# Gate and up products of a Mamba-macaron layer as seven block products

## Chip, core and metric

One NeuronCore of a Trainium2 chip. The metric is the device time of one launch in microseconds; lower is better. Three runs of the kernel before gave a median of 832.96 us (832.76 to 834.3).

## What is computed

One layer on 2048 tokens of width 512, all in float32: `x = x + 0.5 * ffn(layernorm(x))`, `x = x + attn(layernorm(x))`, `x = x + 0.5 * ffn(layernorm(x))`. `ffn` is one 512x512 product with a dequantized int4 weight plus a rank 16 term and a bias. `attn` is a Mamba-2 mixer (16 chunks of 128 tokens, 4 heads) and behind it the part that the change touches:

```
h2 = rmsnorm(h, ln2_w)                                    # 2048 x 512
mlp = silu(h2 @ gate_w.T) * (h2 @ up_w.T) @ down_w.T      # 512 -> 1792 -> 512
return h + mlp
```

## The kernel before

A float32 operand of a large product is held as two float16 parts, high and low, and a product is three matmuls (`product`, `PARTS`: high x high, high x low, low x high) for each 128 of the contracted length. All these matmuls have one line, L1382. Producing a pair of parts takes two instructions: ScalarE copies to float16 (high), VectorE subtracts (low).

The engines run queues that are written out by hand, and wait on semaphores. SyncE issues nearly all transfers.

First come the dequantization, the first ffn and the mixer, chunk by chunk (`step(c)`, c = 0 to 15). In chunk c, GpSimd does `scan_c`, `scan_d` and `rms2` (the root mean square of chunk c, and the addition to the rows `xs`); ScalarE squares (`square`), makes `h2n_p` (`hi2`) and exponentials (`scan_ecs`, L591, which TensorE's `s1_mask`, L1465, waits for); SyncE then transposes h2 into the tile `h2`. The 1792 features are taken as 7 pairs of 256 (p = 0 to 6); a pair's gate and up weights are `raw_gu`, its down weights `raw_d`. The weights are multiplied by `ln2` (`fold`), scaled by a power of two found with GpSimd's `pair_max` (a reduction over partitions, L428), and cut in parts (`cut_a`, `cut_b`: L612, L1069, L783, L1080).

For a pair, `gate_up(p, n)` computes for one of 4 tiles i of 512 tokens and one half x of 128 features the gate and the up product: 24 matmuls into two PSUM banks. Then ScalarE takes tanh (L790), VectorE makes silu and the product of the two (L1297, L1298), and the result is cut in parts (L800, L1304). `down(p, i)` multiplies a tile's 256 features by the down weights: 4 chunks of 6 matmuls, each added to `xs` by one VectorE instruction, L1315. So a pair is 8 x 24 + 16 x 6 = 288 matmuls. Four `gate_up` of pair 0 run inside chunks 12 to 15. `gate_up(0, 5)` is the one that needs the h2 of the last chunk.

At the end comes the second ffn: for each of 16 chunks VectorE's statistics (`c_stats`), GpSimd's `c_norm` and `c_bias`, ScalarE's `c_hi`, VectorE's `c_lo`, a transposing transfer, 12 matmuls (`c_f`) and `c_out`. The last pair's `down` for the tiles 2 and 3 run beside its beginning, the ones for 0 and 1 between its `gate_up`.

Of the kernel before, what the change touches and what calls it, by code (L numbers as in the profile page):

```python
# [14 lines left out]
P = 128  # L15
EPS = 1e-5
ACT_SCALE = 2.0 ** 10
DOWN = ACT_SCALE ** -2
GATED_SCALE = 2.0 ** -54
W_TOP = 14  # L20
# [8 lines left out]
def build(nc, x_in, w_in_t, conv_w, conv_b, a_log, d_skip, dt_bias, w_out_t, ln1_w, ln2_w,  # L29
# [23 lines left out]
    with ctx:  # L53
# [29 lines left out]
        w_dn = [n_T[:, 1024 * p:1024 * (p + 1)].rearrange("p (b n) -> p b n", b=2) for p in range(2)]  # L83

# [18 lines left out]
        state = sb("state", [P, H, P])  # L103

# [23 lines left out]
        d_diag = sb("d_diag", [P, H, P])  # L128
# [80 lines left out]
        def tokens_of(t, c):  # L209
# [30 lines left out]
            sem(n) for n in "e_h2T e_xres e_ncs e_gu e_tanh_g e_silu_g e_gated e_gated_hi".split())  # L240
        e_gated_lo, e_down, e_acc, e_w_gu0, e_w_gu1d, e_w_hi, e_fold, e_wmax = (
# [42 lines left out]
        def _(sp_):  # L284
# [61 lines left out]
            for c in range(NCH):  # L346
                a = c + 2 * CH
                if a + 1 < NCH:
                    t0(a + 1)
                if c > 0:  # L350
                    t2(c - 1)
                if a < NCH:
                    t1(a)
                    next_x(a)
            t2(NCH - 1)
            for p in range(1, NP):
                sp_.wait_ge(e_w_gu1d, p * 2)
                load_pair(p)
# [18 lines left out]
        def _(po):  # L377
# [116 lines left out]
            def step(c):  # L494
# [37 lines left out]
        def _(ac):  # L532
# [134 lines left out]
            def step(c):  # L667
# [35 lines left out]
                if c == 2 * CH + 2:  # L703
                    cut_a(0)
                if c == 2 * CH + 3:
                    cut_b(0)
# [71 lines left out]
            def cut_b(p):  # L778
                if p > 0:
                    ac.wait_ge(e_gu, p * (2 * NS))  # L780
                    ac.wait_ge(e_down, p * (NS * CH))
                hi_gu(1)
                ac.activation(w_dn[0], raw_d[:, :, :], ACT.Copy, scale=sw3[:, 2:3]).then_inc(e_w_hi, 1)  # L783

            def gate(p, n):
                s = p * (2 * NS) + n
                k = order_of(p)[n]
                ac.wait_ge(e_gu, s + 1)
                ac.wait_ge(e_descale, p + 1)
                ac.activation(gt[:, n % 2, :], bank(gu_bank(p, n, 0)), ACT.Tanh, scale=dgh[:, :]).then_inc(e_tanh_g, 1)  # L790
                ac.wait_ge(e_gated, s + 1)
                if k >= NS:
                    i = k - NS
                    if i >= 2:
                        if p * (NS * CH) + (i - 1) * CH > 0:
                            ac.wait_ge(e_down, p * (NS * CH) + (i - 1) * CH)
                    dst = mB[0][:, i % 2, :]
                else:
                    dst = mA[0][:, k, :]
                ac.activation(dst, gp[:, n % 2, :], ACT.Copy).then_inc(e_gated_hi, 1)  # L800
# [6 lines left out]
            def pair(p, nxt):  # L807
                for n in range(EARLY_GU if p == 0 else 0, 2 * NS):
                    gate(p, n)
                    if p > 0 and n == 0:  # L810
                        cut_b(p)
                    if nxt and n == 2 * NS - 2:
                        cut_a(p + 1)

            for p in range(NP):
                pair(p, p + 1 < NP)
# [13 lines left out]
        def _(ve):  # L830
# [362 lines left out]
            def step(c):  # L1193
# [38 lines left out]
                if c == 2 * CH:  # L1232
                    fold(0)
                if c == 2 * CH + 1:
                    maxima_gu()
# [4 lines left out]
                if c == 2 * CH + 3:  # L1240
                    cut_a(0)
# [6 lines left out]
                else:  # L1248
                    if j == 0:
                        cut_b(0)  # L1250
# [470 lines left out]
```

## Time and profile before

| | |
|---|---|
| median of 3 runs | 832.96 us |
| the profiled execution | 831.91 us, of which the span shown is 830.2 us |
| TensorE busy | 95% of the span |
| VectorE, ScalarE, GpSimd busy | 69%, 39%, 23% |
| mixer and the chunks, up to TensorE's last `w(15)` | until 365.8 us |
| seven pairs | until 785.3 us |
| second ffn | until the end |

A row of the timeline has start and duration in us, engine, line, operation, output and inputs, the count, and in brackets the idle time before it with what ended it. A group row has shapes, count, total busy us, the mean ns of one, and the idle time before. Matmuls are pipelined: their distance, and not the length of one, is what a row of many costs.

### The profile page before, as it was taken

The numbers are of one execution on the slowest core, as the hardware profiler recorded it, in microseconds if no ns is written. First come the engines' busy times: TensorE is split into PE (matmuls) and PEld (weight loads), VectorE is DVE, ScalarE is ACT, GpSimd is POOL, SyncE is SP. The second block draws the span as 40 slices with busy tenths as digits, with TensorE's granted clock in tenths as the row PEclk, the third lists the DMA queues.
The fourth block names the chain that finished last, engine by engine and source line by source line (L and its number), as shares of the span: only waits on it lengthen the run. The fifth ranks groups of instructions, "written<-read, shape, count | busy, mean of one in ns | idle before, by whom it ended". The sixth has DMA issues, their size and how long they took to land.

```text
span 830.2 us, 10082 instructions
## 1 busy us (share of the span) xinstructions
PE 791.9 (95%) x3682; PEld 370.2 (45%) x3683; DVE 570.0 (69%) x1088; ACT 326.5 (39%) x633; POOL 188.5 (23%) x243
## 2 busy tenths in 40 slices
PE   7977799999899799999999999999999999999898
PEld 3433354454455344444444444444444444444343
DVE  4799778978868786546557557557557558555885
ACT  2685566766654565432032032032032032031452
POOL 4523344563533143310000000000000000000385
PEclk9999999999999899999999999999999999999999
DMA  8622332231210010112020020020020020000275
GB/s 306 147 49 48 70 62 51 52 89 28 51 25 15 13 26 13 26 30 73 0 77 1 1 76 1 1 77 0 1 77 1 0 77 1 1 0 1 51 179 175
DMA packets 80880, 40.88 MB, mean 49 GB/s; under 512 B 66064, under 2 KB 73232, under 8 KB 80832
## 3 DMA queue, kind: packets, MB, share of 16 engines
q1 hardware_dynamic: 80448, 40.15, 18.6%
q8 instruction: 29, 0.48, 0.3%
q14 instruction: 19, 0.16, 0.1%
q10 hardware_dynamic: 384, 0.10, 0.1%
HBM read 20.32 MB, written 4.19 MB: 30 GB/s over the span
## 4 chain that ended last, share of the span: by engine, by line
PE 58%; DVE 2%; ACT 1%; DMA 1%; SPq 0%; issue 0%; POOL 0%; DVEq 0%
PE PS L1382 54%; PE PS L1510 2%; DMA raw_d<-down_t 1%; PE PS L1500 0%; PE PS L1492 0%; PE PS L1483 0%; PE PS L1475 0%; DVE raw_gu L1045 0%; DVE mx L1049 0%; DVE xs L1315 0%; DVE stage L1298 0%; DVE stage L1297 0%; ACT stage L800 0%; SPq L314 0%; DVE mx L1052 0%
## 5 line engine op out<-in xcount | busy, mean ns | idle before, releaser
L1382 PE MATMUL PS<-h,x_t 128*128 128x512 f16 x1344 | 294.3, 379 | 1.9 <-DMA h<-h2n_p 1.9
L1382 PEld LDWEIGHTS PS<-h,x_t 128*128 128x128 f16 x1344 | 131.4, 98 | 162.4 <-issue 2.9
L1382 PE MATMUL PS<-n_T,stage 128*128 128x512 f16 x672 | 148.6, 379 | 2.7 <-DVE xs L1315 2.7
L790 ACT ACTIVATE stage<-PS,dgh 128x512 f32<-128x512 f32 x56 | 38.5, 687 | 215.1 <-PE PS L1382 214.4
L1382 PE MATMUL PS<-h,w_in 128*128 128x512 f16 x480 | 111.2, 385 | 2.5 <-DMA h<-hn_p 1.4
L1297 DVE SCALAR_TENSOR_TENSOR stage<-stage,PS 128x512 f32<-128x512 f32 x56 | 38.4, 686 | 101.0 <-ACT stage L790 101.0
L1382 PEld LDWEIGHTS PS<-n_T,stage 128*128 128x128 f16 x672 | 65.6, 98 | 82.4 <-issue 3.6
L1315 DVE SCALAR_TENSOR_TENSOR xs<-PS,d_d,xs 128x512 f32<-128x512 f32 x112 | 77.9, 745 | 12.7 <-PE PS L1382 11.7
L800 ACT ACTIVATE stage<-stage 128x512 f16<-128x512 f32 x56 | 35.3, 630 | 117.0 <-DVE stage L1298 117.0
L1382 PEld LDWEIGHTS PS<-h,w_in 128*128 128x128 f16 x480 | 47.3, 99 | 70.3 <-issue 19.6
L428 POOL PARTITION_ALL_REDUCE mxa<-mx x7 | 2.6, 373 | 328.2 <-DVE mx L1052 322.7
L1304 DVE TENSOR_TENSOR stage<-stage 128x512 f16<-128x512 f32 x56 | 38.7, 691 | 36.2 <-ACT stage L800 36.2
L386 POOL TENSOR_TENSOR r<-mv,mhalf 128x1 f32<-128x1 f32 (+1 forms) x32 | 27.2, 852 | 87.1 <-DVE mv L862 68.2
L1382 PE MATMUL PS<-w_ffn,raw_gu 128*128 128x512 f16 x192 | 41.6, 379 | 0.0
L1382 PE MATMUL PS<-w_ffn,n_T 128*128 128x512 f16 x144 | 34.7, 393 | 7.1 <-DVE xs L958 5.4
L1298 DVE SCALAR_TENSOR_TENSOR stage<-stage,PS 128x512 f32<-128x512 f32 x56 | 38.4, 687 | 1.9
L1026 DVE SCALAR_TENSOR_TENSOR raw<-pre,cw,raw 128x512 f32<-128x512 f32 x36 | 29.4, 816 | 9.1 <-ACT raw L631 8.8
L1026 DVE SCALAR_TENSOR_TENSOR stage<-pre,cw,stage 128x512 f32<-128x512 f32 x36 | 29.8, 827 | 5.9 <-ACT stage L631 5.7
L1510 PE MATMUL PS<-w_out,stage 128*128 128x512 f32 x64 | 29.1, 598 | 3.1 <-DVE stage L1001 3.1
L386 POOL TENSOR_TENSOR rC<-mvC,mhalf 128x1 f32<-128x1 f32 x16 | 12.2, 761 | 83.9 <-DVE mvC L864 83.7
L416 POOL TENSOR_TENSOR S<-S,d_diag 128x512 f32<-128x512 f32 x16 | 25.2, 1574 | 26.5 <-DVE S L991 26.5
L1069 DVE SCALAR_TENSOR_TENSOR x_t<-raw_gu,sw,x_t 128x512 f16<-128x512 f32 x28 | 21.8, 820 | 12.6 <-ACT n_T L783 9.4
(199 smaller groups left out, 1031.1 us busy)
## 6 DMA issues: line engine op xcount, KB each, us to landing
x_t<-x_in SPq DMA_DIRECT2D x16, 256.0 KB, 3.0
out<-x_t SPq DMA_DIRECT2D x16, 256.0 KB, 2.3
raw_gu<-gate_t SPq DMA_DIRECT2D x7, 512.0 KB, 4.2
raw_gu<-up_t SPq DMA_DIRECT2D x7, 512.0 KB, 5.3
raw_d<-down_t SPq DMA_DIRECT2D x7, 512.0 KB, 6.0
raw<-w_in_t SPq DMA_DIRECT2D x4, 642.0 KB, 9.5
h<-q_t SPq DMA_DIRECT2D x4, 256.0 KB, 4.9
w_out<-w_out_t SPq DMA_DIRECT2D x1, 1024.0 KB, 13.0
```

Source lines behind the costliest of these rows:

```text
L386: return po.tensor_tensor(dst, src, mhalf[:, 0:src.shape[-1]], ALU.pow)
L416: po.tensor_tensor(S[:, j % 2, :, :], S[:, j % 2, :, :], d_diag[:, :, :], ALU.add).then_inc(e_SD, 1)
L790: ac.activation(gt[:, n % 2, :], bank(gu_bank(p, n, 0)), ACT.Tanh, scale=dgh[:, :]).then_inc(e_tanh_g, 1)
L800: ac.activation(dst, gp[:, n % 2, :], ACT.Copy).then_inc(e_gated_hi, 1)
L1026: ins = ve.scalar_tensor_tensor(xbc[i % 2][:, b, :], pre[:, w, k:k + ST], cw[:, b, k:k + 1], xbc[i % 2][:, b, :], ALU.mult, ALU.add)
L1069: last = ve.scalar_tensor_tensor(w_gu[1][:, g, :, cols], raw_gu[:, g, :, cols], sw3[:, g:g + 1], w_gu[0][:, g, :, cols], ALU.mult, ALU.sub ...
L1297: link(ve.scalar_tensor_tensor(gt[:, w, :], gt[:, w, :], 1.0, bank(gu_bank(p, n, 0)), ALU.add, ALU.mult), e_silu_g, s + 1)
L1298: ve.scalar_tensor_tensor(gp[:, w, :], gt[:, w, :], GATED_SCALE, bank(gu_bank(p, n, 1)), ALU.mult, ALU.mult).then_inc(e_gated, 1)
L1304: ve.tensor_tensor(lo_, gp[:, n % 2, :], hi, ALU.subtract).then_inc(e_gated_lo, 1)
L1315: ve.scalar_tensor_tensor(xs[:, c, :], bank(4 + t), d_d[:, :], xs[:, c, :], ALU.mult, ALU.add).then_inc(e_acc, 1)
L1382: ins = pe.matmul(out_, lhs(a, b, k), rhs(a, b, k), start=first and n == 0, stop=last and n == len(todo) - 1)
L1510: last = pe.matmul(bank(b), y[:, h, (c % CH) * P:(c % CH + 1) * P], w_out[:, h, :], start=h == 0, stop=h == H - 1)
```

## The change

Pair 0 is computed as before. For the pairs 1 to 6, [gate; up] times two token tiles is a 2x2 block product: rows gate and up, contracted halves of 256, columns tile 2u and tile 2u+1. A `unit(m)` (p, half x, u; 4 units for a pair, 24 in all) computes it in 7 products of 6 matmuls instead of 8. The operands that are sums come from GpSimd: `s_adds(p)`, 4 sums of weights for a pair (128x512 float32 each), and `t_op(q, n)`, 4 blocks (q) of 10 steps (n) that make T1 to T4 from h2, once for all pairs; ScalarE (`t_hi`, `hi_st`) and VectorE (`t_lo`, `lo_st`) cut them in parts. VectorE adds the products up: of the 13 VectorE instructions of a unit, 7 have one operand in PSUM and 6 have two in SBUF. The products go round 5 banks, each free again at its addition (`FREE_AT`). `fold` goes to ScalarE, which then also scales the weights in place (`norm`).

The additions to `xs`: ScalarE copies a down product out of PSUM with its scale (`evict`), GpSimd adds it (`x_add`, 128x512). The down products of pair p run in the units of pair p+1 (4 in a unit, 2 in the four units of pair 1), and those of pair 6 behind the last unit, 9 of them ahead of the second ffn and 7 between its chunks; these are added by VectorE as before (`tail`). The load of pair 1 moves ahead into chunk 13, its `fold` to the end of chunk 13, its maxima and `pair_max(1)` to chunk 14. In every later pair `pair_max` stands between the additions to `xs`. Two scale constants are smaller.

The core of the diff:

```diff
+            T_EARLY = {2 * CH + 2: range(0, 3), 2 * CH + 3: range(3, 6), 3 * CH: range(6, 9), 3 * CH + 1: range(9, 10),
+                       3 * CH + 2: range(10, 11), 3 * CH + 3: range(11, 14)}
+            def t_ready(q, r_):
+                if q > 0:
+                    po.wait_ge(e_tlo, 4 * (q - 1) + r_ + 1)
...
+            s_adds(1)
+            for n in range(14, 3 * N_TOP):
+                t_op(n // N_TOP, n % N_TOP)
+            def unit(m):
+                p, n = UNITS[m][0], m % 4
+                ds = downs_of(m)
+                for e, d in enumerate(ds):
+                    x_add(d)
+                    if m < 2 and e == 0:
+                        for k in range(5 * m, 5 * m + 5):
+                            t_op(3, k)
+                if p + 1 < NP:
+                    if n == 1:
+                        pair_max(p + 1)
+                    if n == 2:
+                        s_adds(p + 1)
...
@@ ScalarE, end of a chunk
+                if c == 3 * CH + 1:
+                    fold(1)
+                if c == 3 * CH + 2:
+                    for r_ in range(4):
+                        t_hi(0, r_)
...
@@ VectorE
+            st_a(1)
+            for r_ in range(4):
+                t_lo(1, r_)
+            for m in range(NU):
+                unit(m)
...
@@ TensorE
+            def unit(m):
+                p, x, u = UNITS[m]
+                if x == 0:
+                    pe.wait_ge(e_w_gu0, p + 1)
+                else:
+                    pe.wait_ge(e_w_gu1d, p * 2 + 1)
+                if p == 1:
+                    pe.wait_ge(e_tlo, 8 * (u + 1))
+                ds = downs_of(m)
+                seventh(m, IP1)
+                seventh(m, IP2)
+                down_in_unit(ds[0])
+                seventh(m, IP6)
...
```

The VectorE queue behind pair 0's last `gate_up` (L1618 is `gate_lo`, L1369 to L1373 `lo_st`, L1387 `t_lo`, L1658 and on the additions of unit 0), with the change:

```order
L1611 SCALAR_TENSOR_TENSOR th<-th,PS 128x512 [waits e_tanh_g]
L1612 SCALAR_TENSOR_TENSOR pre<-th,PS 128x512 [waits e_silu_g]
L1618 TENSOR_TENSOR stage<-pre,stage 128x512 [waits e_gated_hi]
L1369 TENSOR_TENSOR n<-raw_gu,n 128x512 [waits e_w_hi]
L1370 TENSOR_TENSOR d_diag<-raw_gu,d_diag 128x256
L1372 TENSOR_TENSOR stage<-w_in,stage 128x256 x2
L1373 TENSOR_TENSOR stage<-raw,stage 128x512
L1387 TENSOR_TENSOR w_in<-hn,w_in 128x512 [waits e_thi]
L1387 TENSOR_TENSOR w_in<-h2n,w_in 128x512 [waits e_thi]
L1387 TENSOR_TENSOR w_in<-n_p,w_in 128x512 [waits e_thi]
L1387 TENSOR_TENSOR w_in<-hn_p,w_in 128x512 [waits e_thi]
L1658 TENSOR_TENSOR Ld<-h2n_p,PS 128x512 [waits e_gu,e_p1]
```

Before, the same place read so (L1304 is `gate_lo`, L1315 the additions of `down`, L1289 to L1291 the scales of pair 1, L1297 its first silu):

```order
L1304 TENSOR_TENSOR stage<-stage 128x512 [waits e_gated_hi]
L1315 SCALAR_TENSOR_TENSOR xs<-PS,d_d,xs 128x512 [waits e_down] x8
L1289 TENSOR_SCALAR dgh<-pw 128x1
L1290 TENSOR_SCALAR d_tmp<-pw 128x1
L1291 TENSOR_SCALAR d_d<-d_tmp 128x1 [waits e_dsx]
L1297 SCALAR_TENSOR_TENSOR stage<-stage,PS 128x512 [waits e_tanh_g]
```

The subtraction that ends pair 0 is now followed by five cuts of weights (in four rows) and four of T operands, and then by the first addition of unit 0; the eight additions to `xs` have left this queue.

The GpSimd queue at the end of the chunks, before (L420, L386 and L424 are `rms2` of chunks 14 and 15, L428 `pair_max`, the bare ISA rows load the code of what follows):

```order
L420 TENSOR_SCALAR ms<-ssq 128x1 [waits e_ssq]
L386 TENSOR_TENSOR r<-ms,mhalf 128x1 [waits e_ms]
L424 TENSOR_TENSOR xs<-xs,x 128x512 [waits e_x2]
L420 TENSOR_SCALAR ms<-ssq 128x1 [waits e_ssq]
L386 TENSOR_TENSOR r<-ms,mhalf 128x1 [waits e_ms]
L424 TENSOR_TENSOR xs<-xs,x 128x512 [waits e_x2]
L428 ISA
L428 ISA mxa<-mx 128x3 [waits e_wmax] x6
```

and with the change (L490, L456, L494 are `rms2`; L603 is `t_op(1, 0)`; L498 `pair_max(1)`):

```order
L490 TENSOR_SCALAR ms<-ssq 128x1 [waits e_ssq]
L456 TENSOR_TENSOR r<-ms,mhalf 128x1 [waits e_ms]
L494 TENSOR_TENSOR xs<-xs,x 128x512 [waits e_x2]
L603 TENSOR_TENSOR hn<-h 128x512 [waits e_tlo,s_h2T]
L498 ISA
L498 ISA mxa<-mx 128x3 [waits e_wmax]
L490 ISA
L490 TENSOR_SCALAR ms<-ssq 128x1 [waits e_ssq]
L456 TENSOR_TENSOR r<-ms,mhalf 128x1 [waits e_ms]
L494 TENSOR_TENSOR xs<-xs,x 128x512 [waits e_x2]
L607 TENSOR_TENSOR h2n<-h 128x512 [waits e_tlo]
```

Between the two `rms2` now stand a T step that waits for VectorE's `t_lo(0, 0)` and `pair_max(1)` with a row of code loading on both sides.

## Rows read from the trace of the kernel before

**Rows 1.** The page's first part: busy us, share of the span, instructions.

```profile
PE 791.9 (95%) x3682; PEld 370.2 (45%) x3683; DVE 570.0 (69%) x1088; ACT 326.5 (39%) x633; POOL 188.5 (23%) x243
```

**Rows 2.** The chain of waits: its longest piece, start us, us, what.

```profile
389.16 383.49 PE PS L1382 x1776
```

**Rows 3.** Windows: busy time of the engines in 60 us amid the pairs.

```profile
480.00:540.00 60.00, 60.00 (x279) 27.20 (x278) 36.82 (x55) 13.33 (x21) 0.37 (x1) 1.00 0.08 27
```

**Rows 4.** Groups by form, whole span: what the durations of the sum come from.

```profile
L1304 DVE TENSOR_TENSOR stage<-stage 128x512 f16<-128x512 f32 x56 | 38.7, 691 | 36.2 <-ACT stage L800 36.2
...
L1017 DVE TENSOR_TENSOR x<-n,PS 128x512 f32<-128x512 f32 x16 | 11.0, 685 | 8.2 <-PE PS L1510 7.7 <-issue 0.6
...
L1080 DVE SCALAR_TENSOR_TENSOR n_T<-raw_d,sw,n_T 128x1024 f16<-128x1024 f32 x7 | 9.0, 1279 | 0.0
...
L935 DVE SCALAR_TENSOR_TENSOR w_in<-raw,lsw,w_in 128x256 f16<-128x256 f32 x4 | 1.7, 476 | 0.0
...
L1049 DVE TENSOR_REDUCE mx<-raw_gu 128x1 f32<-128x1024 f32 x14 | 16.4, 1213 | 0.2
...
L800 ACT ACTIVATE stage<-stage 128x512 f16<-128x512 f32 x56 | 35.3, 630 | 117.0 <-DVE stage L1298 117.0
...
L612 ACT ACTIVATE x_t<-raw_gu,sw 128x512 f16<-128x512 f32 x28 | 18.5, 706 | 0.0
...
L424 POOL TENSOR_TENSOR xs<-xs,x 128x512 f32<-128x512 f32 x16 | 20.3, 1270 | 0.0
```

**Rows 5.** Timeline, VectorE and GpSimd, two SBUF inputs each: chunk 11, and alone.

```profile
322.33 2.42 DVE L1069 SCALAR_TENSOR_TENSOR x_t<-raw_gu,sw,x_t 128x512 f16<-128x512 f32 x2
...
322.48 1.71 POOL L416 TENSOR_TENSOR S<-S,d_diag 128x512 f32<-128x512 f32 x1 [1.14 <-DVE S L991]
...
394.22 1.41 DVE L1069 SCALAR_TENSOR_TENSOR x_t<-raw_gu,sw,x_t 128x512 f16<-128x512 f32 x2 [0.53 <-ACT x_t L612]
```

**Rows 6.** Timeline, the same engines in chunk 13: VectorE's input in PSUM.

```profile
343.87 0.75 DVE L1001 SCALAR_TENSOR_TENSOR raw<-PS,d_ih,raw 128x512 f32<-128x512 f32 x1 [0.86 <-PE PS L1492]
...
344.04 1.27 POOL L424 TENSOR_TENSOR xs<-xs,x 128x512 f32<-128x512 f32 x1
```

**Rows 7.** Timeline of GpSimd around the reduction over partitions, L428.

```profile
281.90 0.39 POOL L428 PARTITION_ALL_REDUCE mxa<-mx  x1 [5.57 <-issue]
...
289.07 0.18 POOL L420 TENSOR_SCALAR ms<-ssq 128x1 f32<-128x1 f32 x1 [6.78 <-issue]
```

**Rows 8.** Windows on TensorE around an idle time: busy, granted clock, DMA.

```profile
282.00:285.00 3.00, 0.94 (x6) 0.69 0.00 0
285.00:288.00 3.00, 3.00 (x5) 0.50 0.00 0
288.00:291.00 3.00, 3.00 (x10) 0.68 0.00 0
```

**Rows 9.** Timeline, end of chunk 13: ScalarE and the matmul that waits.

```profile
343.07 0.58 ACT L591 ACTIVATE ecs<-PS 128x512 f32<-128x512 f32 x1
343.70 0.39 PE L1465 MATMUL PS<-mask_b,ident_b 128*128 128x512 bf16 x1
```

**Rows 10.** Timeline: rms2 of chunks 14 and 15, and gate_up(0, 5).

```profile
356.33 0.19 POOL L420 TENSOR_SCALAR ms<-ssq 128x1 f32<-128x1 f32 x1 [6.42 <-ACT junk L578]
...
367.55 0.19 POOL L420 TENSOR_SCALAR ms<-ssq 128x1 f32<-128x1 f32 x1 [9.17 <-ACT junk L578]
...
373.02 1.25 PE L1382 MATMUL PS<-h,x_t 128*128 128x512 f16 x5 [1.91 <-DMA h<-h2n_p]
```

**Rows 11.** Timeline: statistics of two chunks on VectorE; a wait of TensorE.

```profile
768.38 0.69 DVE L858 BATCH_NORM_STATS2 st<-xs 128x6 f32<-128x512 f32 x1
...
769.39 0.68 DVE L858 BATCH_NORM_STATS2 st<-xs 128x6 f32<-128x512 f32 x1
...
780.08 1.24 PE L1382 MATMUL PS<-n_T,stage 128*128 128x512 f16 x5 [2.27 <-DVE xs L1315]
```

**Rows 12.** Transfers: the transposing ones of the second ffn, us to landing.

```profile
raw_gu<-n_p SPq DMA_TRANSPOSE x4, 2.8
```

More of the change, by code:

```diff
@@ L16 @@
 EPS = 1e-5
[L17 removed]
+ACT_SCALE = 2.0 ** 9
 DOWN = ACT_SCALE ** -2
[L19 to L20 removed]
+GATED_SCALE = 2.0 ** -48
+W_TOP = 12
 TINY = 2.0 ** -90
@@ L355, in _ @@
             t2(NCH - 1)
-            for p in range(1, NP):
+            for p in range(2, NP):
                 sp_.wait_ge(e_w_gu1d, p * 2)
@@ new lines, in fold, with norm @@
+            def fold(p):
+                ac.wait_ge(s_raw, (p + 1) * 48)
+                for k in range(KB):
+                    last = ac.activation(raw_gu[:, :, k, :], raw_gu[:, :, k, :], ACT.Copy, scale=ln2[:, k:k + 1])
+                last.then_inc(e_fold, 1)
+            def norm(p):
+                ac.wait_ge(e_wscale, p + 1)
+                for g in range(2):
+                    last = ac.activation(raw_gu[:, g, :, :], raw_gu[:, g, :, :], ACT.Copy, scale=sw3[:, g:g + 1])
+                last.then_inc(e_norm, 1)
@@ L805, in _ @@
             hi2(NCH - 1, CH - 1)
[L807 to L816, printed above, removed]
+            for n in range(EARLY_GU, 2 * NS):
+                gate(0, n)
+                if n == EARLY_GU:
+                    norm(1)
+                if n == EARLY_GU + 2:
+                    st_a(1)
+            for r_ in range(4):
+                t_hi(1, r_)
+            def unit(m):
+                p, n = UNITS[m][0], m % 4
+                ds = downs_of(m)
+                if m > 0:
+                    hi_s(m - 1, 0)
+                copy_p1(m)
+                if m > 0:
+                    hi_s(m - 1, 1)
+                evict(ds[0])
+                tanh_s(m, 0)
+                evict(ds[1])
+                if n == 0:
+                    st_b(p)
+                if p + 1 < NP:
+                    if n == 1:
+                        fold(p + 1)
+                    if n == 2:
+                        norm(p + 1)
+                    if n == 3:
+                        st_a(p + 1)
+                for d in ds[2:]:
+                    evict(d)
+                if m < 2:
+                    for r_ in range(4):
+                        t_hi(m + 2, r_)
+                tanh_s(m, 1)
+            for m in range(NU):
+                unit(m)
+            hi_s(NU - 1, 0)
+            hi_s(NU - 1, 1)
             def c_hi(c, k):
@@ L1240, in step @@
                 if c == 2 * CH + 3:
-                    cut_a(0)
+                    cut_a()
+                if c == 3 * CH + 2:
+                    maxima_gu(1)
+                    maximum_d()
+                if c == 3 * CH + 3:
+                    for r_ in range(4):
+                        t_lo(0, r_)
                 if i + 1 < NS:
```

552 lines of the change are left out of this document (426 added, 126 removed).

## The prediction

> **What bounds the kernel now.** I read the page first: TensorE is busy 95% of the span, VectorE 69%, GpSimd 23% [rows 1]. The chain of waits then says where: its longest piece is one run of 1776 matmuls in 383.49 us, 0.216 us each, with nothing between [rows 2]. The windows show the same: amid the pairs TensorE is busy all 60 us, VectorE 36.8, ScalarE 13.3, GpSimd 0.4 [rows 3]. So the seven pairs cost what their matmuls cost: a pair is 288 x 0.216 = 62.2 us. What a shorter pair is worth depends on how far the other engines, and the start and end of this stretch, can follow. My sum is made against the profiled execution's own 831.9 us (span 830.2 and 1.7 around it); the median is 1.1 us higher. A measurement of this kernel can tell about 0.2% from no change, 1.7 us.
>
> **Matmuls removed.** 24 units of 42 instead of 48: 144 x 0.216 = **-31.1 us**. A unit with four down products is 66 matmuls, 14.3 us, a pair 57.0; the four units of pair 1, with two each, take 11.7 us apiece.
>
> **Chunks 12 to 15.** At the end of chunk 13 ScalarE goes straight from `square` to the exponentials of chunk 15, and TensorE's mask matmul starts 0.05 us after these [rows 9]. `fold(1)` now stands between: 4 instructions like L612 (0.706, overlapping to 0.67) [rows 4], so **+2.7 us**. Its weights, ordered behind the low part of chunk 12, I take as landed. The other early steps fit into idle time there.
>
> GpSimd is worse. Around the one `pair_max` amid other work it stood still for 5.57 us before and 6.78 us after, released by nothing shown [rows 7]; that is the price of the two rows of code loading. `pair_max(1)` now stands between `rms2` of chunks 14 and 15, behind T step (1,0), which waits for VectorE's `t_lo(0,0)`. The `rms2` of chunk 14 started at 356.33 [rows 10], now 359.0, with ScalarE's square just done. From there four `t_hi` at 0.63 and `hi2(14)` end at 362.3 on ScalarE, `lo2(14)` and the state update (some 1.9) at 364.2 on VectorE, `t_lo(0,0)` at 364.9, the T step at 366.2. Then 5.57 + 0.39 + 6.78: the last `rms2` starts at 379.0, not 370.2 (367.55 [rows 10] plus 2.7). Queued behind it are the last h2, its transpose and `gate_up(0,5)`, which waited for this chain already [rows 10]: **+8.8 us**, if loading doesn't start earlier; 5.0 if the T step doesn't wait. TensorE is then idle for over 10 us. After a window with only 0.94 us of work in 3 its granted clock went to 0.5, the 1.2 GHz level: three windows at 0.69, 0.50 and 0.68 lose about 3 us [rows 8]. I add **+2.5**.
>
> **From pair 0 to unit 0.** Let G be the end of `gate_up(0,7)`. In its shadow nothing is ready: tanh G+0.9, two VectorE instructions G+2.3, high part G+3.0, low part G+3.7; then `st_a(1)`, five cuts (two of 512 elements at 0.69; three of 256, which I take at 0.42 since L935 of that size took 0.476 with a scalar operand [rows 4]) to G+6.5; then four `t_lo` at 0.72, all of which unit 0 awaits. That is G+9.3. But each `t_lo` also releases GpSimd's next T step, and the two engines shut each other out: two L1069, 1.41 us when alone, took 2.42 around a GpSimd addition, which itself took 1.71 [rows 5] instead of 1.27 [rows 4], while an instruction with an input in PSUM ran its 0.75 beside such an addition at 1.27 [rows 6]. With two steps let in, unit 0 starts at **G+12**.
>
> **Units 0 and 1.** T blocks 2 and 3 are made now: 20 GpSimd steps. The trace has no such step on float16 inputs; the nearest row is the float32 addition, 1.27 us (1.3 apart) [rows 4]; half of it, for half the bytes, is the other end. I use 1.27, since it has two inputs of as many elements. (The Trainium skill, GPSIMD Engine Reference, section 3.1, counts about 2.6 cycles an element for a float32 addition and puts it down to two inputs that share one read port; by that rule a float16 step would cost the full price, and the third rival below would lose one of its conditions. No row here can tell.) Block 2 runs to G+24.5; in unit 0 VectorE also waits for ScalarE's `st_b(1)`, cuts 3.9 us of weights and four `t_lo`, to G+38. Block 3, with additions between and VectorE's 0.7 us between steps, ends near G+56, and the last `t_lo` at G+60. Unit 2 waits for it, where two units of matmuls alone end at G+23.3: **+36.8 us** with the start. The lower bound is VectorE alone: 2 x 13 x 0.72 + 3.9 + 3.6 (maxima) + 8 x 0.7 = 31.8 behind the first products at G+12: +20.6.
>
> **Units 2 and 3** are held by VectorE as in the next part, less two additions each: 32 us instead of 23.3, of which 0.9 is lag that is no loss: **+7.9**.
>
> **Pairs 2 to 5.** VectorE has 52 instructions at 0.69 (0.72 apart), 37.4 us; cuts 2 x 2.65 + 1.28 (L1080), maxima 3.6 (L1049) [rows 4] and scales 1.5 (seven small ones), together 49.1 us without a single wait. The five PSUM banks let it lag by six or seven us before TensorE stops. GpSimd has 16 additions and 4 `s_adds`, 25.4 us, against 35 VectorE instructions with two SBUF inputs. Laid out unit by unit with lock and order: n=3: 9.4 + cuts 2.7 + lock 7.7 (the four `s_adds` fall on silu and the low parts, two additions on the cuts) = 19.8. n=0: 9.4 + 3.9 + lock 3.6 + 1.2 for ScalarE's high parts = 18.1. n=1: 9.4 + 3.6 + 1.6 = 14.6. n=2: 9.4 + 1.5 + 1.6 = 12.5. Sum 65.0 against 57.0 of matmuls: 4 x 8.0 = **+32**. What the one row of a meeting cannot say is whether each costs the later engine all that is left of the other. The Trainium skill does (SBUF — State Buffer, "SBUF: two separate sides"): a lock, held for a whole instruction, taken by VectorE instructions with two SBUF inputs; by it a pair is the 65 laid out, without it 57.0, and the row agrees. Bounds: 0 if the meetings fall into idle time, +52 (70 a pair) if each GpSimd instruction costs its whole 1.27 somewhere and code loading pushes `s_adds` later. Pair 6 has no next pair to prepare: 0.
>
> **The end.** All 16 down products of pair 6 now come behind the units. VectorE first finishes the last unit (4.4 us), then needs 0.75 + 1.01 + gaps, 1.95 us, for each chunk's addition and statistics [rows 11] where TensorE needs 1.3 for the product, and has four banks. Five of these and the first `c_lo` end at +14.9; its transpose, 2.8 to landing [rows 12], makes the second ffn start at +18.2, where nine products alone end at +11.7. From there TensorE bounds again (3.9 a chunk against 3.4). 6.7 us idle against the 2.3 of now [rows 11]: **+4.4**.
>
> **Sum:** 831.9 - 31.1 + 2.7 + 8.8 + 2.5 + 36.8 + 7.9 + 32 + 4.4 = 895.9; 897 on the scale of the median.
>
> **Rivals.**
> First: TensorE stays the bound of pairs 2 to 5. For it: VectorE's 49.1 is 8 us short of 57.0, and meetings in idle time cost nothing. Against it: three heavy units follow each other. Without 32, and with units 2 and 3 at +2: 859; 843 to 873 with the bounds of the start.
> Second: the clock falls in the steady pairs too. A unit that waits for its weights leaves TensorE idle for 5 us, longer than the idle time of [rows 8]; at half clock the products of the next unit come late enough to hold VectorE. 3 us twice a pair adds 24: 921.
> Third, faster than before: the handover is covered. It takes T steps at 0.65 us, code that loads ahead of its place, and no lock wait on the path. Then 831.9 - 31.1 + 2.7 + 20.6 + 3 = 827. It decides where T block 3 ends ahead of VectorE's own work and a pair's VectorE time stays under 57.0. For it: only single meetings are shown. Against it: it needs all three, and even then the bound of 20.6 stands.
>
> **Chances.** Forecast (873 to 912) 0.57; first rival 0.24; second 0.09; third 0.07; between the first and third 0.03. The range from 843 to 930 holds all but the third rival and the last few of the second. Faster by over 0.2%: 0.07; within: 0.02; slower: 0.91.
>
> **What would show it.** Right: TensorE idle for some 10 us before `gate_up(0,5)` with GpSimd idle on no releaser before L498 and L490; idle for 10 to 12 us before unit 0 and again before unit 2, released by `t_lo` (L1387); matmul groups of the pairs waiting on VectorE's L1682 or on the cuts; low parts and silu with a mean well above 0.69 (some 1.1). Wrong: windows amid the pairs with TensorE busy 60 of 60; VectorE's SBUF instructions at 0.69; a T step under 1 us; the last `rms2` at its old distance from its square.

## The result and the profile after

The changed kernel takes 882.42 us (median of 4, 881.53 to 883.72), the one before 832.86 us (831.82 to 834.3): ratio 1.0595, 95% interval 1.0574 to 1.0616. The profiled execution took 883.72 us (span 882.0).

The page's first part, which answers to [rows 1]:

```profile
PE 780.5 (88%) x3538; PEld 359.6 (41%) x3539; DVE 669.4 (76%) x1208; ACT 438.6 (50%) x833; POOL 408.8 (46%) x395
```

144 matmuls fewer, and TensorE is busy for only 11.4 us less, since part of the rest ran at the half clock; its share of the span falls from 95% to 88%. Where it stands idle is told by the rows of its timeline that begin behind a wait (start, duration, and in brackets the idle time and its releaser), from the last chunk on:

```profile
385.67 7.09 PE L1748 MATMUL PS<-h,x_t 128*128 128x512 f16 x24 [11.75 <-DMA h<-h2n_p]
421.75 5.21 PE L1748 MATMUL PS<-h,n 128*128 128x512 f16 x12 [8.28 <-DVE w_in L1387]
438.25 2.76 PE L1748 MATMUL PS<-h,x_t 128*128 128x512 f16 x12 [2.22 <-DVE x_t L1373]
464.48 4.33 PE L1748 MATMUL PS<-h,n 128*128 128x512 f16 x12 [13.84 <-DVE raw L1387]
492.08 4.20 PE L1748 MATMUL PS<-h,n 128*128 128x512 f16 x12 [2.55 <-DVE stage L1373]
555.82 4.75 PE L1748 MATMUL PS<-h,n 128*128 128x512 f16 x12 [5.14 <-DVE stage L1373]
620.20 4.98 PE L1748 MATMUL PS<-h,n 128*128 128x512 f16 x12 [5.25 <-DVE stage L1373]
684.91 5.06 PE L1748 MATMUL PS<-h,n 128*128 128x512 f16 x12 [5.33 <-DVE stage L1373]
750.37 4.76 PE L1748 MATMUL PS<-h,n 128*128 128x512 f16 x12 [6.01 <-DVE stage L1373]
826.53 4.23 PE L1748 MATMUL PS<-w_ffn,raw_gu 128*128 128x512 f16 x12 [3.40 <-DMA raw_gu<-n_p]
```

Three long single waits lie at the handover: for h2 of the last chunk, for the T operands of unit 0 (L1387, `t_lo`), and for those of unit 2. From then on TensorE stops once a pair at the pair's first unit, for 2.55 us the first time and for 5 to 6 us after that, and what it waits for is the last of VectorE's cuts of the new weights (L1373). Twelve matmuls take 2.76 us at the full clock; behind nearly all these waits they take 4.2 to 5.2. A window there shows the granted clock at the lower level; the other row is a whole pair (columns: the stretch, its length, busy time of TensorE, of its weight loads, of VectorE, ScalarE, GpSimd, then the clock):

```profile
555.80:558.80 3.00, 2.98 (x8) 1.06 (x9) 2.97 (x6) 0.72 (x1) 0.00 (x0) 0.50 0.00 0
546.40:610.80 64.40, 59.26 (x266) 26.33 (x265) 52.03 (x74) 31.88 (x53) 29.99 (x22) 0.95 0.08 25
```

VectorE is busy for 52.0 of the 64.4 us. It is not full: it stands idle for 12 us of each pair, and is late all the same. The chain of waits goes another way, over GpSimd. In a pair (start, us, what):

```profile
592.74 0.58 POOL mxa L498
...
600.68 6.31 POOL xs L655 x4
606.99 1.70 POOL w_in L639
608.69 1.68 POOL raw L640
610.38 1.67 POOL w_in L642
```

Around the reduction over partitions GpSimd stands still, as in [rows 7]; behind it come four additions to `xs`, and only then the four sums of weights. GpSimd's, ScalarE's and VectorE's own rows at that place:

```profile
592.74 0.58 POOL L498 PARTITION_ALL_REDUCE mxa<-mx  x1 [6.27 <-issue]
600.68 1.26 POOL L655 TENSOR_TENSOR xs<-xs,n 128x512 f32<-128x512 f32 x1 [7.36 <-issue]
...
613.43 0.72 ACT L974 ACTIVATE stage<-w_in 128x256 f16<-128x256 f32 x2 [3.10 <-POOL raw L644]
...
614.71 1.70 DVE L1369 TENSOR_TENSOR n<-raw_gu,n 128x512 f16<-128x512 f32 x1 [3.19 <-ACT stage L975]
616.33 1.48 DVE L1370 TENSOR_TENSOR d_diag<-raw_gu,d_diag 128x256 f16<-128x256 f32 x1
617.73 1.82 DVE L1372 TENSOR_TENSOR stage<-w_in,stage 128x256 f16<-128x256 f32 x2
```

Two causes stand in these rows, one behind the other. ScalarE waits 3.10 us for the last sum, and VectorE for ScalarE. Then VectorE's cuts take 1.70 and 1.48 us instead of 0.69 and 0.42, beside GpSimd's next additions. The prediction had the second as the bound of a pair; the experiments ask how much is the first.

### The profile page after: what moved, and what is told of

The parts are those of the page before. It is cut to its first block, busy times and chain, and to the rows that moved or that the text cites. A ratio compares the mean times of both kernels' runs of the same rounds, so it can differ in the third digit from the quotient of the medians.

```text
span 882.0 us, 10714 instructions
## 1 busy us (share of the span) xinstructions
PE 780.5 (88%) x3538; PEld 359.6 (41%) x3539; DVE 669.4 (76%) x1208; ACT 438.6 (50%) x833; POOL 408.8 (46%) x395
## 4 chain that ended last, share of the span: by engine, by line
issue 20%; PE 19%; POOL 15%; DVE 4%; ACT 1%; DMA 1%; POOLq 0%; ACTq 0%; DVEq 0%
PE PS L1748 19%; POOL xs L655 10%; POOL w_in L639 1%; POOL raw L640 1%; POOL w_in L642 1%; POOL hn L603 1%; DVE xs L1695 0%; DVE st L1138 0%; PE PS L1876 0%; DVE w_in L1387 0%; DMA h<-h2n_p 0%; DMA raw_gu<-n_p 0%; DVE stage L1372 0%; DVE n L1369 0%; DVE raw L1387 0%
## 5 line engine op out<-in xcount | busy, mean ns | idle before, releaser
L655 POOL TENSOR_TENSOR xs<-xs,x 128x512 f32<-128x512 f32 x59 | 84.8, 1445 | 110.3 <-ACT x L1039 81.4
L1748 PE MATMUL PS<-h,x_t 128*128 128x512 f16 x408 | 95.0, 384 | 14.0 <-DMA h<-h2n_p 11.8
L1748 PE MATMUL PS<-h,n 128*128 128x512 f16 x144 | 47.1, 495 | 46.4 <-DVE stage L1373 24.3
L1748 PE MATMUL PS<-n_T,stage 128*128 128x512 f16 x288 | 70.7, 379 | 1.4 <-DVE S L1687 0.8
L456 POOL TENSOR_TENSOR r<-mv,mhalf 128x1 f32<-128x1 f32 (+1 forms) x32 | 27.3, 852 | 87.1 <-DVE mv L1142 68.2
L1748 PEld LDWEIGHTS PS<-h,x_t 128*128 128x128 f16 x408 | 40.2, 99 | 65.6 <-DMA h<-h2n_p 12.2
L655 POOL TENSOR_TENSOR xs<-xs,n 128x512 f32<-128x512 f32 x29 | 40.9, 1410 | 49.3 <-ACT n L1039 41.8
L1039 ACT ACTIVATE x<-PS,d_d 128x512 f32<-128x512 f32 x59 | 39.9, 677 | 42.6 <-PE PS L1748 28.1
L1748 PE MATMUL PS<-pre,stage 128*128 128x512 f16 x192 | 49.3, 379 | 0.0
L1748 PEld LDWEIGHTS PS<-n_T,stage 128*128 128x128 f16 x288 | 27.9, 98 | 36.5 <-DVE xs L1695 1.9
L1748 PE MATMUL PS<-w_in,x_t 128*128 128x512 f16 x144 | 34.8, 379 | 0.4 <-DVE Ld L1658 0.4
L490 POOL TENSOR_SCALAR ms<-ssq 128x1 f32<-128x1 f32 x16 | 3.1, 191 | 65.5 <-ACT junk L744 51.6
```

The source lines that it names most:

```text
L456: return po.tensor_tensor(dst, src, mhalf[:, 0:src.shape[-1]], ALU.pow)
L490: po.tensor_scalar(ms[:, c:c + 1], ssq[:, c:c + 1], DOWN / DM, EPS * DOWN, ALU.mult, ALU.add).then_inc(e_ms, 1)
L655: po.tensor_tensor(chunk_of(xs, c), chunk_of(xs, c), d_tmps[d % 3], ALU.add).then_inc(e_xadd, 1)
L1039: ac.activation(d_tmps[d % 3], bank(5 + d % 3), ACT.Copy, scale=d_d[:, p % 3:p % 3 + 1]).then_inc(e_ev, 1)
L1748: ins = pe.matmul(out_, lhs(a, b, k), rhs(a, b, k), start=first and n == 0, stop=last and n == len(todo) - 1)
```

## The experiments

Times are medians, beside runs of the kernel before on the same chip. I call theory A that of the prediction for the pairs (VectorE's own work and the meetings with GpSimd), theory B the chain reduction, additions, sums, cuts.

**e1_no_reduction**: the reductions of pairs 2 to 6 out.

```diff
                     if n == 1:
-                        pair_max(p + 1)
+                        po.wait_ge(e_wmax, p + 2)
+                        po.sem_inc(e_wmax_all, 1)
```

> GpSimd's reductions over partitions for the pairs 2 to 6 are left out; their weights are scaled by the power of two of pair 1 (a part of the computation that is changed: the scale no longer follows each pair's own maximum). With them goes the time of 13.6 us a pair in which GpSimd stood still around the reduction (6.27 before it and 7.36 behind it). All additions on GpSimd stay, so all meetings with VectorE stay. Theory A (the pairs are held by VectorE's own 49 us and by waits for the lock that it shares with GpSimd's additions): 64.4 us a pair become 62 to 64, in all 872 to 880. Theory B (TensorE stops once a pair, 5.2 us, for VectorE's cuts, which wait for ScalarE's, which wait for the four sums of weights on GpSimd, which stand behind the reduction and the additions that it delays): the waits of 24.3 us in all on the cuts go, and so does what the clock loses behind them (2 us a pair): 882.4 - 24.3 - 10 = 848, between 845 and 855, and a pair of 57 to 58 us.

Measured: 864.7 us, ratio 1.0385 (1.0356 to 1.0415): -17.7 us, between the two. A pair takes 59.2 us where the clock stays up (one pair's first unit starts at 552.21 and the next pair's at 611.39), and 59.6 in the mean of the pairs 2 to 5, against 64.6 in the changed kernel:

```profile
552.21 2.76 PE L1749 MATMUL PS<-h,n 128*128 128x512 f16 x12 [2.07 <-DVE stage L1374]
611.39 2.76 PE L1749 MATMUL PS<-h,n 128*128 128x512 f16 x12 [2.03 <-DVE stage L1374]
670.60 4.45 PE L1749 MATMUL PS<-h,n 128*128 128x512 f16 x12 [2.05 <-DVE stage L1374]
```

(In the profiled execution the chunks ended 3 us later than in the changed kernel's, which hides a part of it in the total. The traces of e3, e4 and e8 show the same, by 1.6 to 3.8 us at `gate_up(0, 5)`; the cause was not looked into.) So 3.1 to 4.0 us of each wait was the chain behind the reduction. Some 2 us of clock went with it in two of the four pairs, where the twelve matmuls take 2.76 us; behind the other two waits, of 2.05 and 2.06 us, they still take 4.45 and 4.14. And the 2 us of waiting stay. VectorE's rows ahead of one, beside the sums, and ScalarE's copy of a sum, which waits for nothing, read:

```profile
595.88 1.60 DVE L1635 SCALAR_TENSOR_TENSOR S<-xds,S 128x512 f32<-128x512 f32 x1
597.41 1.75 DVE L1637 SCALAR_TENSOR_TENSOR xds<-xds,tm 128x512 f32<-128x512 f32 x1
...
605.22 0.71 ACT L975 ACTIVATE stage<-w_in 128x256 f16<-128x256 f32 x2
```

**e4_sums_first**: the same chain, shortened by order alone.

```diff
+                if n == 2 and p + 1 < NP:
+                    s_adds(p + 1)
                 for e, d in enumerate(ds):
                     x_add(d)
...
-                    if n == 2:
-                        s_adds(p + 1)
```

> In the third unit of each pair GpSimd makes the four sums of weights ahead of the unit's four additions to xs, not behind them; the same work, the reductions stay. Theory A (VectorE's time and the lock): no change within 3 us, since the same instructions meet: 880 to 885. Theory B (TensorE waits once a pair for the chain reduction, additions, sums, cuts): the sums come 6.3 us earlier and the cuts with them, which covers the wait of 5.2 us; less the clock's 2 us a pair that is 5 x 7 = 35 at most: 850. Between: the additions come 6.9 us later instead, ScalarE's copies out of PSUM wait for them and stop TensorE at the down products: 865.

Measured: 885.15 us, ratio 1.0619 (1.0594 to 1.0643): no gain. In its trace the pair's wait for the cuts falls to 2.0 to 3.7 us, and another appears ahead of it: TensorE waits 1.3 to 2.4 us at a down product for ScalarE's copy out of PSUM, which waits for GpSimd's late additions.

```profile
615.26 0.82 PE L1748 MATMUL PS<-n_T,stage 128*128 128x512 f16 x3 [1.86 <-ACT x L1039]
623.02 2.76 PE L1748 MATMUL PS<-h,n 128*128 128x512 f16 x12 [3.71 <-DVE stage L1373]
```

Theory A's number, and not its reason: GpSimd is behind by the 14 us of the reduction, and the order mostly chooses who waits for it. In the trace the pairs 2 to 5 do get 1.3 us shorter each (63.25 instead of 64.6), which the chunks, 3.8 us later there, hide in the total. That the three buffers between ScalarE and GpSimd are too few for 14 us is argued from this; more buffers were not tried.

**e8_no_sums**: as e1, and the sums out too.

```diff
                 base = (p - 1) * 4
+                if p > 1:
+                    po.wait_ge(e_norm, p)
+                    po.sem_inc(e_sadd, 4)
+                    return
```

> As e1_no_reduction (the reductions of the pairs 2 to 6 left out), and also the four sums of weights of the pairs 2 to 6 left out, so that their products take the sums of pair 1 (computation left out). The 2.05 us that TensorE still waits in each pair there is, by the theory of the lock, what the four sums cost VectorE where they meet its silu, low parts and cuts (1.60, 1.75, 1.64 and 1.76 us instead of 0.69): a pair becomes 57.1 us, in all 864.7 - 5 x 2 = 855. By the other theory (VectorE has simply too much to do between the units, lock or not) the wait stays: 862 to 865.

Measured: 852.95 us, ratio 1.0228 (1.0201 to 1.0254): 11.75 us less than e1. Amid the pairs TensorE is busy for all 60 of 60 us, which a faster sum chain cannot explain, since ScalarE did not wait for the sums in e1 either:

```profile
552.00:612.00 60.00, 60.00 (x280) 27.19 (x279) 50.98 (x79) 34.24 (x57) 21.87 (x16) 1.00 0.08 27
594.98 0.69 DVE L1639 SCALAR_TENSOR_TENSOR S<-xds,S 128x512 f32<-128x512 f32 x1
```

A pair takes 57.0 us here, what its matmuls cost. So the 2 us, with the clock that e1 loses behind two of the waits, are the meetings of the four sums with VectorE's silu and low parts, which are 0.69 us long again. The sixteen additions a pair, which still stretch a cut here and there, cost TensorE nothing: they fall where VectorE has time.

**e2_max1_after**: `pair_max(1)` behind the last `rms2`.

```diff
                 rms2(c, c % CH)
+                if c == NCH - 1:
+                    pair_max(1)
...
-                if c == NCH - 2:
-                    pair_max(1)
```

> pair_max(1) moves behind rms2 of chunk 15 on GpSimd; nothing else. Both theories: the last rms2 no longer waits for the two idle times around the reduction, gate_up(0, 5) starts at 373 instead of 385.7, and TensorE's idle time of 11.8 us there goes (with about 2 us of clock behind it). GpSimd's part of T block 1 still ends near 403, and unit 0 cannot start before 405, so 12 to 15 us of the 14 are kept: 868. Rival: VectorE now waits in its queue for the maxima (scales(1) stands behind gate_up(0, 4)), and gate_up(0, 5) and (0, 6) pay for it: 876.

Measured: 871.62 us, ratio 1.0464 (1.044 to 1.0488): -10.8 us, between the two numbers. TensorE's wait for the last h2 is 1.89 us, as before [rows 10], not 11.75. From `rms2` of chunk 14 to `gate_up(0, 5)` it takes 16.7 us (360.90 to 377.56), as before (356.33 to 373.02); in the changed kernel 26.5.

**e3_t_early**: the T operands cut between pair 0's last `gate_up`s and ahead of unit 0; block 3 made ahead of the additions.

```diff
-            for n in range(14, 3 * N_TOP):
+            for n in range(14, 4 * N_TOP):
                 t_op(n // N_TOP, n % N_TOP)
...
@@ VectorE (ScalarE alike)
+                if n == EARLY_GU + 1:
+                    t_lo(1, 0)
+                    t_lo(1, 1)
+                if n == EARLY_GU + 2:
+                    st_a(1)
+                    t_lo(1, 2)
+                    t_lo(1, 3)
+            for r_ in range(4):
+                t_lo(2, r_)
-            st_a(1)
-            for r_ in range(4):
-                t_lo(1, r_)
```

> The T operands are made earlier: the cuts of block 1 stand between the last gate_ups of pair 0, those of block 2 ahead of unit 0 and those of block 3 in unit 0, and GpSimd makes block 3 ahead of the units' additions. If the start of the units is held by this chain alone, unit 0 starts 2.5 us behind gate_up(0, 7) instead of 8.3, and unit 2 right behind unit 1 (13.8 us of waiting go): 882.4 - 6 - 13.8 - 3 (clock at half behind the two idle times) = 860. If what holds VectorE there is the lock with GpSimd's twenty steps, these still meet VectorE's additions of unit 0 and 1, only earlier, and half comes back: 870.

Measured: 871.33 us, ratio 1.0456 (1.0429 to 1.0483): -11.1 us, the rival's number. Unit 0 starts 2.3 us behind the last `gate_up`, and unit 2 without a wait (0.62 us come inside it). What comes back is a wait of 6.65 us ahead of unit 1 (2.22 in the changed kernel), for the cuts of `st_b(1)`; VectorE's four cuts of block 2 ran against GpSimd's steps:

```profile
418.80 1.64 DVE L1389 TENSOR_TENSOR raw<-hn,raw 128x512 f16<-128x512 f32 x1
420.37 1.64 DVE L1389 TENSOR_TENSOR raw<-h2n,raw 128x512 f16<-128x512 f32 x1
```

**e5_dma_max, e6_dma_max_t_early**: no reduction on GpSimd at all, and the scales as exact as before.

```diff
+            def spread_max(p):
+                sp_.wait_ge(e_wmax, p + 1)
+                if p > 0:
+                    sp_.wait_ge(s_mxr, p * 16)
+                sp_.dma_start(mx_d[:, :], mx3[:, :]).then_inc(s_mxw, 16)
+                sp_.wait_ge(s_mxw, (p + 1) * 16)
...
+                sp_.dma_start(mxb[:, :], mx_d.rearrange("(o p) n -> o (p n)", o=1).broadcast_to([P, P * 3])).then_inc(s_mxr, 16)
...
+                ve.tensor_reduce(mxa3[:, :], mxb[:, :].rearrange("p (q n) -> p n q", n=3), AX_X, ALU.max).then_inc(e_wmax_all, 1)
```

> The changed kernel with all its maxima spread over the partitions by two small transfers (128x3 to HBM and back to every partition) and one VectorE reduction of 384 elements; GpSimd's partition_all_reduce is gone and with it every idle time around it. Same results as the kernel's own. From the two runs before: -17.7 us in the pairs (what leaving five reductions out gave), -11 at pair_max(1), and some 4 at the reduction of chunk 9, where TensorE's windows show an idle time and a clock of 0.5: 882.4 - 17.7 - 11 - 4 = 850, between 846 and 856. Rival: two transfers in a row take longer than the 13 us of GpSimd, or VectorE waits for them in its queue: 865 or more.

> As e5_dma_max, with the T operands made early as in e3_t_early. The two gains are in different stretches and should add: 850 - 11 = 839, between 834 and 846. If so this is still behind the kernel before (833): what is left is VectorE's lock waits in units 0 to 3 and 2 us a pair. Rival: with the reductions gone, T blocks and rms2 run into each other and the second gain shrinks: 846.

Measured: 849.51 us (ratio 1.0202, 1.0181 to 1.0224) and 841.1 us (1.0111, 1.0067 to 1.0155). The second gain shrinks a little beside the first: 8.4 us, of the 11.1 that e3 brought alone; unit 0 starts after a wait of 4.63 us in e6, of 2.31 in e3. The transfers take 2.1 and 3.9 us to landing:

```profile
mxb<-mx_d SPq DMA_DIRECT2D x7, 192.0 KB, 3.9
mx_d<-mx SPq DMA_DIRECT2D x7, 1.5 KB, 2.1
```

**e7_before_dma_max, e11_before_dma_later**: the control, the kernel before with these transfers, and then with VectorE's scales one `gate_up` later.

```diff
-                    if nxt and n == NS + 1:
+                    if nxt and n == NS + 2:
                         scales(p + 1)
```

> Control: the kernel before with the same transfers in place of its reductions. Its pairs are bound by TensorE in any case, so only the reduction of chunk 9 can pay: TensorE's 2 us of idle time at 282 and the 3 us that the clock costs behind it: 828, between 826 and 832. If the reductions were no cost at all there: 833.4. It says against what e5 and e6 have to be held.

> The control once more: the kernel before with maxima by transfers, and VectorE's scales one gate_up later in its queue (in e7_before_dma_max VectorE waited there for 6.5 us of transfers with the additions to xs queued behind, which stopped TensorE for 2.9 us a pair). The pairs are then bound by TensorE again: 832, between 829 and 834, no faster than with GpSimd's reductions, since in the kernel before nothing waits for them in the pairs. If moving it is not enough: 840 or more.

Measured: 854.01 us (1.0254, 1.023 to 1.0279), and 831.98 us (0.9988, 0.9977 to 0.9998). The first was a miss of mine. I had counted a transfer as free; but the step that waits for it stood at its old place in VectorE's queue, and VectorE idled with a pair's additions behind it:

```profile
521.98 0.67 DVE L1070 TENSOR_REDUCE mxa<-mxb 128x3 f32<-128x384 f32 x1 [3.55 <-DMA mxb<-mx_d]
```

TensorE waited 20.1 us in all for those additions (7 times, the last for 2.27 us as in the kernel before [rows 11]). One place later only that last wait is left, and the kernel before gains 0.1%: its reductions cost it next to nothing, and the 33 us (882.4 to 849.5) that the changed kernel gained from their removal are the change's own.

**e9_two_plain, e10_two_plain_split, e12_retimed**: can seven products pay? Pair 1 with eight products, so that all T operands are made beside pairs 0 and 1.

```diff
+        PP = 2
+        G2 = 2 * NS * PP
-        UNITS = [(p, x, u) for p in range(1, NP)
+        UNITS = [(p, x, u) for p in range(PP, NP)
-        DOWNS = [(0, c) for c in range(2 * CH, NCH)] + [(p, c) for p in range(1, NP - 1) for c in range(NCH)]
+        DOWNS = [(PP - 1, c) for c in range(2 * CH, NCH)] + [(p, c) for p in range(PP, NP - 1) for c in range(NCH)]
...
+            for n in range(4 * N_TOP):
+                t_op(n // N_TOP, n % N_TOP)
+            s_adds(PP)
```

> Pair 1 too is computed with eight products, as pair 0; only the pairs 2 to 6 take seven. The T operands are then made and cut during pair 0 and pair 1, where VectorE has over 20 us a pair to spare, and nothing of the change is left in the chunks. Maxima by transfers as in e5_dma_max. If the losses of the changed kernel outside the steady pairs are what the experiments say (T chain, pair_max(1)), these go: 831.9 - 5 x 3.0 (a pair of 59.2, as measured without the reductions, against 62.2) + 4.4 (end) + 2.5 (start of the units and clock) = 824, between 819 and 830: faster than the kernel before. Rival: the twenty-four more matmuls (5.2 us) and GpSimd's forty steps beside VectorE's pair 1 cost as much as they save: 833 or more.

> As e9_two_plain, and the two cuts of the next pair's weights that need no sums (1.1 us on VectorE) move from the fourth unit of a pair to the end of the third. VectorE's work is the same. If the wait that is left at each pair's start is VectorE being behind in the fourth unit (three silu or low-part instructions at 1.6 to 1.76 beside the four sums, then the cuts), the wait shrinks by 1.1 to 2 us in each of four pairs: 5 us less than e9_two_plain. If it is ScalarE or GpSimd that is late there, nothing changes.

Measured: 847.5 us (1.0168, 1.0153 to 1.0182) and 842.64 us (1.0122, 1.0096 to 1.0148). The first missed by 23 us. TensorE waited 2.7 us for VectorE at a down product of pair 0, and 0.8, 0.5 and 6.2 us in pair 1. I had taken VectorE to have over 20 us to spare: it has them, but not at every place. And its later pairs take 60.8 to 61.1 us, not 59.2: their wait is 2.25 us, and behind it the twelve matmuls take 4.45 us, at a clock of 0.53, as in two of e1's four pairs:

```profile
593.84 4.45 PE L1795 MATMUL PS<-h,n 128*128 128x512 f16 x12 [2.25 <-DVE stage L1402]
593.80:596.80 3.00, 2.96 (x8) 1.09 (x9) 2.97 (x5) 0.72 (x1) 0.00 (x0) 0.53 0.00 0
```

The split takes the wait to 1.6 us, the matmuls are at 2.76 again, and a pair at 58.75: -4.9 us as expected, and 6.8 between the profiled executions: 0.6 us of wait and 1.7 of clock for each of three pairs. The 0.6 is the split's. That the clock stayed up may be in part luck, since it did so even behind the wait of 3.16 us here:

```profile
534.64 2.76 PE L1814 MATMUL PS<-h,n 128*128 128x512 f16 x12 [3.16 <-DVE stage L1418]
593.40 2.76 PE L1814 MATMUL PS<-h,n 128*128 128x512 f16 x12 [1.61 <-DVE stage L1418]
```

The split itself is this:

```diff
                 ve.tensor_tensor(u3[k], u3[k], p_bank(m, IP4), ALU.subtract).then_inc(e_add, 1)
+                if p + 1 < NP and n == 2:
+                    ve.wait_ge(e_norm, 2 * (p + 1 - PP) + 1)
+                    lo_g(0)
```

Last, the misplaced steps of pair 1 put where VectorE stands idle:

```diff
-        T_CUTS = {(0, 5): ((0, 0), (0, 1)), (0, 6): ((0, 2), (0, 3)), (0, 7): ((1, 0), (1, 1)),
-                  (1, 0): ((1, 2), (1, 3)), (1, 1): ((2, 0), (2, 1)), (1, 2): ((2, 2), (2, 3)),
-                  (1, 3): ((3, 0), (3, 1)), (1, 4): ((3, 2), (3, 3))}
+        T_CUTS = {(0, 5): ((0, 0), (0, 1)), (0, 6): ((0, 2), (0, 3)),
+                  (0, 8): ((1, 0), (1, 1), (1, 2), (1, 3)), (1, 0): ((2, 0), (2, 1)), (1, 1): ((2, 2), (2, 3)),
+                  (1, 4): ((3, 0), (3, 1)), (1, 6): ((3, 2), (3, 3))}
...
-                if n == 3:
+                if n == 2:
                     fold(2)
```

(the keys are pair and `gate_up`, (0, 8) behind the last additions of pair 0; the values the blocks' cuts; and `st_b(2)` moves to the start of unit 0.)

> As e10_two_plain_split, with VectorE's and ScalarE's steps moved out of the places where TensorE waited for them there: the four cuts of T block 1 stand behind the last additions of pair 0 (VectorE stood still for 5 us there) and no longer ahead of them (2.7 us of TensorE), no T cut stands beside the maxima of pair 1 (1.3 and 6.2 us, and 1.7 of clock behind the latter), and the second half of pair 2's weights is cut at the start of unit 0, where VectorE waits for the first products (2.2 us and 1.7 of clock). All of it kept: 842.6 - 15 = 827, faster than the kernel before. If VectorE's queue only moves the waits (pair 1 is then VectorE-bound as well): 835 or more. If half is kept: 833 to 836, no faster than the kernel before.

Measured: 831.14 us, the kernel before beside it 834.29: ratio 0.9967, 0.9956 to 0.9978. Faster than the kernel before by an interval that leaves out 1, though by 0.33% alone (single executions overlap: 829.43 to 833.9 against 832.36 to 835.45), and 4 us short of the 827 expected. Left over in its trace are 3.7 and 1.6 us of waiting in pair 1, 2.3 ahead of unit 0, and these:

```profile
521.57 4.15 PE L1822 MATMUL PS<-h,n 128*128 128x512 f16 x12 [3.16 <-DVE stage L1422]
582.89 4.21 PE L1822 MATMUL PS<-h,n 128*128 128x512 f16 x12 [2.68 <-DVE stage L1422]
643.35 2.76 PE L1822 MATMUL PS<-h,n 128*128 128x512 f16 x12 [1.86 <-DVE stage L1422]
```

## Why the prediction was right, step by step

The forecast (897 us, 843 to 930, slower) holds, 14.6 us too high. Made against the profiled executions, its sum was 895.9 and the time 883.7. A part of this closeness is luck: the term of the pairs 2 to 5 nearly has its number, but by two causes, of which one was not in the sum.

| term | forecast | measured |
|---|---|---|
| matmuls | -31.1 | -31.1 |
| `fold(1)` in chunk 13 | +2.7 | +2.8 |
| `pair_max(1)` before the last `rms2` | +8.8 | +9.8 |
| clock behind it | +2.5 | +1.3 |
| from pair 0 to unit 2 | +36.8 | +28 |
| units 2 and 3 | +7.9 | +4.3 |
| pairs 2 to 5 | +32 | +30 |
| pair 6 | 0 | +2 |
| the end | +4.4 | +4.4 |

**Chunks.** `rms2` of chunk 14 starts at 359.14 instead of 356.33 and `gate_up(0, 5)` at 385.67 instead of 373.02; the rest of 12.65 is `pair_max(1)`. GpSimd's rows are those forecast, the T step behind `t_lo` included:

```profile
364.31 2.67 POOL L603 TENSOR_TENSOR hn<-h 128x512 f32<-128x512 f16 x1 [3.10 <-DVE w_in L1387]
...
372.79 0.38 POOL L498 PARTITION_ALL_REDUCE mxa<-mx  x1 [5.81 <-issue]
...
380.17 0.18 POOL L490 TENSOR_SCALAR ms<-ssq 128x1 f32<-128x1 f32 x1 [7.00 <-issue]
```

e2 took it away and gave 10.8 us back. The idle time ahead of a reduction was 5.81 to 6.27 us in the changed kernel's seven. The Trainium skill (GPSIMD Engine Reference, section 2.1) states "approximately 6 µs" for the first call of freshly loaded code; the rows agree, and show that as much again, 6.82 to 7.36 us, passes between a reduction and GpSimd's next instruction.

**From pair 0 to unit 2** was the term mis-sized most. Unit 0 starts at G+8.3, not G+12: the lock took nothing from VectorE there. Its cuts ran at 0.69 us, and it was GpSimd's first step that took 2.67 instead of the 1.15 of the next one. I had charged VectorE for a meeting that GpSimd paid for. In e3 four such cuts took 1.64 each. Who pays at a meeting changed from place to place; forecast as a charge on VectorE it was an upper bound here. Unit 2 starts at G+51, not G+60; the T steps were 1.15 to 1.6 us, but for the first of a block, so the choice of 1.27 for float16 inputs was right, and half of it would have been wrong:

```profile
419.76 0.69 DVE L1387 TENSOR_TENSOR w_in<-h2n,w_in 128x512 f16<-128x512 f32 x1
419.99 2.67 POOL L603 TENSOR_TENSOR hn<-h 128x512 f32<-128x512 f16 x1 [17.35 <-DVE w_in L1387]
420.36 0.69 DVE L1387 TENSOR_TENSOR w_in<-n_p,w_in 128x512 f16<-128x512 f32 x1
...
422.62 1.15 POOL L607 TENSOR_TENSOR h2n<-h 128x512 f32<-128x512 f16 x1
427.53 1.27 POOL L618 TENSOR_TENSOR h2n<-h2n,n_p 128x512 f32<-128x512 f32 x1
```

**Pairs 2 to 5** had the right number for a partly wrong reason, which is luck. I laid VectorE out as full, 65.0 us a pair, and it came to 64.6 with VectorE idle for 12. The sign that I had named for it, silu and low parts with a mean of some 1.1 us, stayed away: a unit's six instructions with two SBUF inputs, which these are, have a mean of 0.86 us in these pairs. The step that failed is the one where GpSimd's queue entered only through the lock: "code loading pushes `s_adds` later" stood among the bounds, not in the sum. Shown by the runs: of the 7.6 us that a pair is over 57.0 in the mean, 4.9 go with the reduction (e1; 3.4 of waiting, the rest clock) and 2.6 with the meetings of the four sums (e8; 2.05 of waiting, most of the rest clock). The second rival, clock falling in the steady pairs, had 3 us twice a pair; it came once, for 2 us, inside the likeliest case. The first rival (TensorE bound) is what e8 shows once both causes are gone.

**The end** has the number forecast, with smaller parts exchanged: 17.0 us from the last unit to the second ffn instead of 18.2, 11.7 of them matmuls, its last wait the first transpose (3.40), and then 1.5 us of clock that the forecast did not have, the thirteenth matmul starting 4.1 us behind the first instead of 2.6.

## What to carry to other kernels

Before handing work to an engine that has time on average, look for its longest uninterruptible stretch and compare it with the buffers between it and its consumers: here the 14 us around a reduction, against three buffers, cost 4.9 us a pair, and the meetings of the four sums 2.6. A step moved or replaced must be placed by who is queued behind it: a transfer that cost nobody anything in one kernel cost 20 us at an unchanged place in another's queue. An algebraic saving of 26 us of matmuls (five pairs of 24 in e12; the change's six would save 31) paid 3 us here, and only after the reductions had left GpSimd and most new dependencies had been put where their engine stood idle.

## What the runs showed of the hardware

A wait of TensorE of some 2 us may cost another 1.7, and its length does not tell whether it does. In e1 four pairs begin behind waits of 2.07, 2.03, 2.05 and 2.06 us: the twelve matmuls then take 2.76, 2.76, 4.45 and 4.14 us, with a granted clock of 0.61 in the 3 us from 670.60 and of 1.00 in those from 611.40. In e4 two waits of 3.71 us differ in the same way (the thirteenth matmul starts 2.60 us behind the first at 623.02, 5.09 at 748.77), and waits of 3.16 us in e10 and e12 (2.76 and 4.15). What told them apart was not tried.

The meeting of VectorE and GpSimd on SBUF is paid by either: VectorE 1.60 to 1.76 us instead of 0.69 beside the sums in e1, GpSimd 2.67 instead of 1.15 at 419.99 in the changed kernel. The Trainium skill (SBUF — State Buffer, "SBUF: two separate sides") says of the lock that whichever starts first holds it for its whole instruction; these rows agree, on both sides. They show one thing more: in e1 the two engines took turns, while GpSimd's step at 419.99 ended only 1.0 us behind the last of three VectorE cuts (419.76, 420.36 and 420.96) that ran at their 0.69 us. A GpSimd addition of 128x512 with float16 inputs takes 1.15 us, with float32 inputs 1.27.
